# A written-out ramp for a fused attention and expert-FFN layer, with another order in its first four steps

## The reference

```
x = x + attention(layernorm(x), ctx, mask)     # x: 4 x 1024 x 256, ctx: 4 x 64 x 256
x = x + ffn(layernorm(x))

attention: q = query @ Wq + bq (16 heads of 16); k = ctx @ Wk + bk; v = ctx @ Wv + bv (one head, shared)
           softmax(q k / 4, masked) @ v, then @ Wo + bo
ffn:       xm = mix of each row with its two neighbours (3 taps per column)
           scores = tanh(xm @ Wo1 + bo1) @ Wo2 + bo2; expert = argmax over 9
           out = layernorm(x + (xm @ W1[expert] + b1[expert]) @ W2[expert] + b2[expert]) * gamma + beta
```

## Time and profile before

| | us |
|---|---|
| median of 3 runs | 359.27 |
| lowest and highest | 357.69, 359.3 |
| profiled execution, device time | 357.65 |
| its span | 355.8 |

### The profile page before, as it was taken

How to read it: one execution, slowest core, us unless ns; L and a number is a source line. 1 busy time by engine, 2 the same in 40 slices (tenths; PEclk the granted TensorE clock), 3 DMA queues, 4 the chain that set the end, 5 groups by cost and what they waited for, 6 DMA issues and landing times.

```text
span 355.8 us, 7313 instructions
## 1 busy us (share of the span) xinstructions
PE 312.0 (88%) x2700; PEld 230.7 (65%) x2700; DVE 282.4 (79%) x606; ACT 183.0 (51%) x285; POOL 188.2 (53%) x226
## 2 busy tenths in 40 slices
PE   1588788765999999999999999999999999799990
PEld 1374364452667957795678767876678568677980
DVE  2675398595769899889989898989798866689866
ACT  1452835625764477537851777258444752367400
POOL 0444002633178179944895299728881787164044
PEclk9998999996999999999999999999999999899996
DMA  7509500020002001200110010000100010001003
GB/s 210 177 0 218 106 0 1 2 76 0 0 4 76 0 2 62 73 3 0 59 52 22 0 59 0 0 0 2 61 0 2 2 61 2 0 0 62 3 0 118
DMA packets 20564, 13.44 MB, mean 38 GB/s; under 512 B 10097, under 2 KB 20282, under 8 KB 20538
## 3 DMA queue, kind: packets, MB, share of 16 engines
q1 hardware_dynamic: 18898, 12.53, 12.0%
q10 hardware_dynamic: 1640, 0.57, 0.7%
HBM read 8.90 MB, written 4.19 MB: 37 GB/s over the span
## 4 chain that ended last, share of the span: by engine, by line
PE 76%; DVE 12%; ACT 5%; issue 3%; POOL 2%; DMA 1%; DVEq 0%; ACTq 0%; POOLq 0%
PE ps L429 16%; PE ps L434 7%; PE ps L584 7%; PE ps L668 6%; PE ps L673 5%; PE ps L669 5%; PE ps L541 5%; PE ps L566 4%; PE ps L560 4%; DVE mx L1115 3%; DVE osb L1139 3%; PE ps L650 2%; PE ps L544 2%; PE ps L635 2%; PE ps L481 2%
## 5 line engine op out<-in xcount | busy, mean ns | idle before, releaser
L1408 POOL TENSOR_TENSOR rs<-ve,halfneg 128x4 f32<-128x4 f32 x24 | 26.7, 1113 | 106.8 <-DVE ve L1078 106.8
L843 ACT ACTIVATE e<-ps 128x1024 f32<-128x1024 f32 x32 | 31.1, 1024 | 20.3 <-PE ps L548 20.3
L1115 DVE TENSOR_REDUCE mx<-ps 128x16 f32<-128x1024 f32 x32 | 37.9, 1216 | 0.3 <-PE ps L516 0.3
L668 PE MATMUL ps<-w2h,hmh 128*128 128x256 f32 (+1 forms) x140 | 35.6, 288 | 0.0
L669 PE MATMUL ps<-w2l,hmh 128*128 128x256 f32 (+1 forms) x140 | 34.7, 283 | 0.0
L1465 POOL TENSOR_TENSOR hml<-hs,hmh 128x512 fp32r<-128x512 f32 x24 | 30.3, 1276 | 7.4 <-ACT hmh L904 7.3
L868 ACT ACTIVATE xh<-x,vb,rs 128x256 f32<-128x256 f32 x32 | 16.6, 591 | 33.5 <-POOL vb L1421 33.5
L584 PE MATMUL ps<-wo,osb 128*128 128x256 f32 x128 | 31.3, 390 | 2.0 <-DVE osb L1139 2.0
L894 ACT ACTIVATE hs<-ps,b1s 128x512 f32<-128x512 f32 x28 | 19.3, 689 | 24.4 <-PE ps L434 24.4
L1454 POOL TENSOR_TENSOR y<-xh2f,gms 128x256 f32<-128x256 f32 x28 | 22.2, 824 | 17.5 <-DVE xh2f L1087 17.5
L429 PE MATMUL ps<-xmh,w1h 128*128 128x512 f32 x80 | 27.8, 429 | 3.3 <-DVE xmh L1190 3.3
(11 more groups left out here) (161 smaller groups left out, 787.5 us busy)
## 6 DMA issues: line engine op xcount, KB each, us to landing
xin<-in_x SPq DMA_DIRECT2D x8, 512.0 KB, 4.1
out<-y SPq DMA_DIRECT2D x7, 512.0 KB, 2.9
min_<-in_mask_Bx1xSxS_ik SPq DMA_DIRECT2D x8, 128.0 KB, 4.8
hs<-in_L_ffn_W SPq DMA_DIRECT2D x2, 288.0 KB
y<-in_constants SPq DMA_DIRECT2D x1, 512.0 KB, 8.7
hs<-in_L_ffn_W SPq DMA_DIRECT2D x1, 512.0 KB
out<-xin SPq DMA_DIRECT2D x2, 256.0 KB, 2.2
cst<-in_constants SPq DMA_DIRECT2D x1, 384.0 KB, 6.0
```

Of the source, the lines that this page charges most:

```text
L668: nc.tensor.matmul(o, L.hi(m, r)[:, ks], w2h[0:r, m, :], start=(m == 0), stop=False)
L843: nc.scalar.activation(e[:, 2 * i:2 * i + 2, :], ps[:, bank:bank + 2, :], ACT.Exp).then_inc(s_e, 1)
L1115: v.tensor_reduce(mx[:, k, :].rearrange("p (a h) -> p a h", a=2), ps[:, bank:bank + 2, :].rearrange("p a (h s) -> p a h s", s=SK), AX.X, A ...
L1408: g.tensor_tensor(ln[7][:, :], ln[6][:, :], halfneg[:, :], ALU.pow).then_inc(s_r, 1)
```

## The change

It has these parts.

1. Start. ACT's queue loads Wq second, and bq is on a semaphore of its own. DVE takes the first layernorm's statistics ahead of the copies of the transposed context; ACT normalises two of the four tiles of chunk (0, 0) and DVE the other two. PE runs `t1(0, 0)` ahead of `keys()`, the mask last; DVE copies the keys after `x_lo`.
2. Step 1. `wq(0, 1)` and, on DVE between the second and the third maximum, `x_lo(0, 1)` move here from step 2 and from the end of the step.
3. FFN weights. SP issues their loads ahead of `next_inputs(0, 0)`. ACT's split of them goes from the end of step 2 to between the two exponential halves of step 2, and DVE's low parts from behind step 2 to its front.
4. Step 3. DVE applies the second layernorm of (0, 0) and (0, 1), at the ends of steps 2 and 3, in place of ACT. `early_mix` goes from the end of step 3 to its front, its high part behind `layernorm1_apply` on ACT and its low part on POOL ahead of `add_beta` and `add_bo`. On PE `wq(1, 0)` and `t2(0, 0)` keep their places ahead of the second scores; `t2(0, 1)` leaves the end of the step.
5. Step 4. PE runs scores half 0, `wq(1, 1)`, `t2(0, 1)` into banks 6 and 7, scores half 1 and only then `w1`. ACT copies the `t2` transposes, then makes the second exponentials and the query copy, and the `hidden` copies come behind them. DVE makes the last column behind the statistics of (2, 0).
6. All four engines' hardware loops are written out.

```diff
...
                 sp.wait_ge(s_ln1, at(b, NJ, j + 1))
+                if (b, j) == (0, 0):
+                    sp.wait_ge(s_ln1d, 1)
                 sp.wait_ge(s_xb, at(b, NJ, j + 1))
                 sp.dma_start(xin[:, j], xr[:, b + 1, j]).then_inc(s_x[j], 16)
...
+            load_ffn_weights()
             next_inputs(0, 0)
-            load_ffn_weights()
...
+            def mask_transposed(b, j, mask_bank):
...
+            def t1(b, j, bank, mask_bank=2):
+                first = (b, j) == (0, 0)
+                if first:
+                    pe.wait_ge(s_ln1d, 1)
+                else:
+                    mask_transposed(b, j, mask_bank)
                 pe.wait_ge(s_ln1, at(b, NJ, j + 1))
                 if mask_bank == 2:
...
+                if first:
+                    mask_transposed(b, j, mask_bank)
...
+            def wq(b, j, bank, first_f=False):
                 pe.wait_ge(s_xTl, at(b, NJ, j + 1))
-                if bank == 0:
+                if first_f:
+                    pe.wait_ge(s_x1, at(b, 2 * NJ, 2 * j - 2))
+                elif bank == 0:
                     pe.wait_ge(s_x2T, at(b, NJ * KD, (j - 1) * KD))
...
-            def t2(b, j, front, late):
+            def t2(b, j, bank=0):
                 pe.wait_ge(s_x1, at(b, 2 * NJ, 2 * (j + 1)))
-                if late:
-                    pe.wait_ge(s_nT, at(b, NJ, j + 2))
...
                 if n:
                     scores_transposed(*n, 0, front)
+                if late:
+                    wq(*front, fb, f)
+                    t2(*late, 6 if f else 0)
+                    scores_transposed(*n, 1, front)
                 if f:
                     w1(*f, 0)
                     w1(*f, 4)
+                if n and not late:
                     scores_transposed(*n, 1, front)
-                if front:
+                if front and not late and n != (0, 0):
                     wq(*front, fb)
-                if late:
-                    t2(*late, front, True)
-                if n and not f:
-                    scores_transposed(*n, 1, front)
                 if not n:
...
                     scores_for_max(*front, 2, banks)
                     scores_for_max(*front, 3, banks)
+                if not n:
+                    wq(*after, fb)
                 if n:
                     project_out(*n, (0, 1))
                 if f:
...
-                if n and (f or n[1] == NJ - 1):
-                    t2(*n, front, False)
+                if f:
+                    t2(*n)
...
             context_transposed()
+            t1(0, 0, 6)
             keys()
-            t1(0, 0, 6)
...
-            with pe.Fori(1, B - 1) as r:
-                step((r, 0), (r, 1), (r - 1, 0), (r + 1, 0))
+            for r in range(1, B - 1):
+                step((r, 0), (r, 1), (r - 1, 0), (r + 1, 0), (0, 1) if r == 1 else None)
                 step((r, 1), (r + 1, 0), (r - 1, 1), (r + 1, 1))
...
             load(ctx_in, ctx.rearrange("b s d -> s b d"), s_ctx)
+            load(wq32, Wq.rearrange("(c p) n -> p c n", p=P), s_wq)
             load(wk[:, :, :], Wk.rearrange("(c p) n -> p c n", p=P), s_wk)
             load(wv[:, :, :], Wv.rearrange("(c p) n -> p c n", p=P), s_wk)
             load(bks[:, :], bk.rearrange("(h p o) -> h p o", h=1, o=1).broadcast_to([P // DK, DK, 1]), s_wk)
             load(bvs[:, :], row_broadcast(bv, DK), s_wk)
-            load(wq32, Wq.rearrange("(c p) n -> p c n", p=P), s_wq)
-            load(bqs[:, :], bq.rearrange("(c p) -> p c", p=P), s_wq)
+            load(bqs[:, :], bq.rearrange("(c p) -> p c", p=P), s_bq)
...
-                for k in range(NT):
+                for k in range(NT // 2 if (b, j) == (0, 0) else NT):
...
                 if n:
                     softmax_exp(*n, 0)
+                if late and f:
+                    copy_t2(*late, 6)
+                    softmax_exp(*n, 1)
+                    q_copy(*front, 0)
+                elif late:
+                    copy_t2(*late)
+                    softmax_exp(*n, 1)
+                    q_copy(*front, 6)
                 if f:
                     hidden(*f, 0)
                     hidden(*f, 4)
-                if late:
-                    layernorm2_apply(*late)
-                    copy_t2(*late)
-                if n:
-                    softmax_exp(*n, 1)
-                if front:
-                    q_copy(*front, 0 if f else 6)
+                if n and n == (0, 0):
+                    split_ffn_weights()
+                if not late:
+                    if n:
+                        softmax_exp(*n, 1)
+                    if front:
+                        q_copy(*front, 0 if f else 6)
...
                 if after and not f:
                     layernorm1_apply(*after)
-                if n and n[1] == 0 and not f:
-                    split_ffn_weights()
+                if late and not f:
+                    early_mixed_hi(n[0])
...
-                if n and not f and n[1] == NJ - 1:
-                    layernorm2_apply(*n)
-                if n and (f or n[1] == NJ - 1):
+                if f:
                     copy_t2(*n)
-                if n and n[1] == NJ - 1 and not f:
-                    early_mixed_hi(n[0])
                 if after and f:
...
+            def first_layernorm1_upper():
+                dve.wait_ge(s_ln1b, 1)
+                for k in range(NT // 2, NT):
+                    a = v.tensor_scalar(xh1[:, k, :], xin[:, 0, k, :], ln1[7][:, k:k + 1], ln1[5][:, k:k + 1], ALU.mult, ALU.add)
+                a.then_inc(s_ln1d, 1)
+
+            def layernorm2_apply(b, j):
+                dve.wait_ge(s_ln2b, at(b, NJ, j + 1))
+                for k in range(NT):
+                    a = v.tensor_scalar(xh2[:, j, k, :], x1[:, j, k, :], ln2[7][:, k:k + 1], ln2[5][:, k:k + 1], ALU.mult, ALU.add)
+                a.then_inc(s_ln2, 1)
...
-            def step(n, front, f, after):
+            def step(n, front, f, after, late=None):
                 banks = banks_for_max(n, f)
-                if after and not f:
+                if after:
                     layernorm1_stats(*after)
-                if after and f:
-                    layernorm1_stats(*after)
+                if n and n == (0, 0):
+                    ffn_weights_lo()
+                if late and f:
+                    last_column(late[0])
+                elif late:
+                    dve.wait_ge(s_wf, 16 * WF_LOADS)
+                    early_mix(late[0])
                 if f and f[1] == 0:
                     second_mix(f[0])
...
+                if not n:
+                    x_lo(*after, 6)
...
-                if after:
+                if after and n:
                     x_lo(*after, 0 if f else 6)
                 if f:
                     layernorm3_apply(*f)
-                elif n and n[1] == NJ - 1:
-                    dve.wait_ge(s_wf, 16 * WF_LOADS)
-                    early_mix(n[0])
-                    last_column(n[0])
-
+                elif n:
+                    layernorm2_apply(*n)
+
+            layernorm1_stats(0, 0)
             transposed_context_copied()
-            layernorm1_stats(0, 0)
+            first_layernorm1_upper()
             memsets()
             key_weights_repeated()
-            keys()
             wq_lo()
             x_lo(0, 0, 6)
+            keys()
             step(None, (0, 0), None, (0, 1))
             step((0, 0), (0, 1), None, (1, 0))
-            ffn_weights_lo()
-            step((0, 1), (1, 0), None, (1, 1))
-            with dve.Fori(1, B - 1) as r:
-                step((r, 0), (r, 1), (r - 1, 0), (r + 1, 0))
+            step((0, 1), (1, 0), None, (1, 1), (0, 0))
+            for r in range(1, B - 1):
+                step((r, 0), (r, 1), (r - 1, 0), (r + 1, 0), (0, 1) if r == 1 else None)
                 step((r, 1), (r + 1, 0), (r - 1, 1), (r + 1, 1))
...
+                if n and n[1] == NJ - 1 and not f:
+                    early_mixed_lo(n[0])
...
-                elif n and n[1] == NJ - 1:
-                    early_mixed_lo(n[0])
...
```

More of the change, by code:

```diff
@@ L210, in layer_program @@
         s_ctx, s_wk, s_wq = sem("context_loaded"), sem("key_value_weights_loaded"), sem("wq_loaded")
+        s_bq = sem("bq_loaded")
         s_wo_in, s_wf = sem("wo_loaded"), sem("ffn_weights_loaded")
@@ L225, in layer_program @@
         s_ln3v, s_ln3r, s_ln3 = sem("ln3_var"), sem("ln3_rstd"), sem("ln3_done")
+        s_ln1d = sem("first_ln1_upper_tiles")
         s_mb, s_xb = sem("mask_bias"), sem("x_plus_bo")
@@ L594, in t2 @@
                     for k in range(NT):
-                        mm = nc.tensor.transpose(ps[:, c, k * P:(k + 1) * P], xh2[:, j, k, c * P:(c + 1) * P], ident)
+                        mm = nc.tensor.transpose(ps[:, bank + c, k * P:(k + 1) * P], xh2[:, j, k, c * P:(c + 1) * P], ident)
                     mm.then_inc(s_x2p, 1)
@@ L802, in _ @@
             load(bvs[:, :], row_broadcast(bv, DK), s_wk)
[L803 to L804 removed]
```

(22 more changed lines are left out.)

3 lines of the change are left out of this document (removed).

## The result

The changed kernel takes 347.35 us (median of 4 runs, 345.63 to 349.92), against 358.48 us for the kernel before on the same chip (4 runs, 354.67 to 359.3). The ratio on record is 0.9707, with a 95% interval of 0.9666 to 0.9748: faster by 2.9% (the quotient of the two medians alone is 0.969). The forecast was 349.8 us in 346.5 to 354.0. The profiled execution took 348.3 us with a span of 346.5, where the forecast for it, without the 0.8 for the median, was 349.05. Its span is 9.3 us shorter than the 355.8 of before.

A forecast was written before the change was run, and what follows sets the result against it. PE was taken to bound the kernel from 97 us on, behind a ramp where no engine is full. -0.6 + 1.9 + 1.3 + 6.0 = 8.6 off 357.65 gives 349.05; plus 0.8, 349.8 us, range 346.5 to 354.

The forecast's parts named there:

- The start (A): Start through step 1, to the transposed maxima of (0, 0): a loss of 0.6 us, at best a gain of 1.3.
- The rival of the start that loses more: Start: Wq's load takes turns with x, which lands at 9.5; a loss of 2.9 us, time 352.1; 7 in 100.
- Step 2 (B): Transposed maxima to second exponentials of step 2: 6.98 us instead of 8.86, a gain of 1.9.
- a rival that would come after the change: Step 2: with wq gone PE has gaps and its clock falls, costing about 3 us, time 353; 13 in 100.
- The second layernorm (C): Step 3: with the layernorm on DVE, PE's 1.34 us wait for ACT before t2(0, 0) goes; a gain of 1.3.
- Step 4 (D): Step 4's new order brings the gate to 92.5 from 98.52: a gain of 6.0 us, 7.0 if hidden weren't behind.
- The loops (E): Hardware loops written out: taken as 0, with bounds 0 and a gain of 0.3 us in all.
- The median: Median of runs was 1.6 us above the profiled run before; half of it, 0.8, was added to the forecast.
- The best bound of the prediction: Whole kernel: 346.0 us from the profiled run if the start gains 1.3, step 4 7.0 and the loops 0.3.
- POOL did come later: Early low part delays POOL's additions and the load of x(2, 0); 2 us lost, time 351.8; 13 in 100.
- The slower case: Clock stays low from step 2 through step 3; slower than before, 370 if all of it; 4 in 100.

The follow-up runs named there:

- e2: Changed kernel with the late transposes, their copies and the last column back at the end of step 3, step 4 in old order; 351.2 us, ratio 0.9805.
- e1: Kernel before with only its four hardware loops written out; 358.46 us, ratio 0.9997.
- e9: Changed kernel with the second layernorm of (0, 0) on ACT again, that of (0, 1) staying on DVE; one run, 348.3 us.
- e12: Changed kernel with the old start and with wq(0, 1) back between the scores of step 2; one run, 349.56 us.
- e7: Changed kernel with ACT's split of the FFN weights moved from between step 2's exponential pairs to the end of step 1; one run, 346.2 us.
- e3: Changed kernel with ACT's copies of the late transposes put behind the second exponentials and query copy in step 4; 353.83 us, ratio 0.9878.
- e10: Changed kernel with the early mix back at the end of step 3, step 4 keeping its new order; one run, 354.43 us.
- e4: Changed kernel with hidden copies 0 and 4 ahead of the query copy in step 4; one run, 348.71 us.
- e11: Changed kernel executed once more, nothing changed; one run, 348.75 us.
- e8: Changed kernel with ACT's weight split at the end of step 1 and the first two hidden copies ahead of step 4's query copy; 346.59 us, ratio 0.9687.
- e5: Changed kernel with the old start: old load order, context copies, first layernorm on ACT, keys ahead of t1; one run, 349.92 us.
- e6: Changed kernel with wq(0, 1) back in step 2 ahead of the second scores and x_lo(0, 1) behind step 1's maxima; one run, 349.1 us.

## Why the prediction was right

**The start (A), predicted -0.6, measured -0.3.** x was there at 6.49, not at 7.2 as taken, and the keys ended at 15.7, not at 16.4. The rival of the start that loses more did not come. By the rule of the Trainium skill, DMA: Bandwidth & Descriptors, Queues, rings and completion order, Wq as the second load of ACT's queue should take turns with x. Of the start's two x loads the faster landed in 5.3 us and the slower in 8.8, where the kernel before had 5.4 and 8.3, and e2, with the new order of loads too, 5.3 and 7.8: a cost of such turns isn't seen on the first load, and nothing waits for the second. The 0.3 measured is itself no more than the difference between two executions: the transposed maxima come at 28.30 and 28.95 with the old start (before, e1), and at 28.59 to 29.03 with the new one, but for e9's 29.46, where a low clock lies ahead of them.

**Step 2 (B), predicted +1.9, measured +1.9, for a reason that was only half right, and so in part by luck.** The new chain was 6.95 us by the trace against 6.98 worked out. But I took the 8.86 us of before as what the order costs. Of it some 1.5 us were work at the lower clock: 3.51 us to the first exponentials against 2.45, and 1.19 us for the product's first pair against 0.73. The measured gain is mostly that this is gone (e12). I had that clock in view as a rival that would come after the change, and did not see that it stood in the term I subtracted from. The price of the split, 0.85, was wrong as well: it is 0.15 to 0.3, since PE needs 2.17 us behind the first exponentials and not 1.65 (e7). The row of the scores with their banks free, 1.14, does not stand for the same scores behind a wait for banks, 2.04. The sum held because the split and PE's chain end together. It is the reading of one execution, too: with the changed kernel's program up to there the chain took from 6.69 (e3) to 7.63 us (e10), by where the low clock lay, which makes B anything from 1.2 to 2.2.

**The second layernorm (C), predicted +1.3, measured +1.4**, and 1.2 when it was undone (e9).

**Step 4 (D), predicted +6.0, measured +6.1.** The third `w1` waited 0.85 for `hidden` where 1.0 was predicted, and e4 shows that it was this and nothing else. The gate is 14.9 us behind `t1`'s start, where it was 21.1. Some 0.9 of the 6.1 are clock here as well: before, the late transposes ran in 1.94 us, with the clock low from 80.4 to 87.2, and the copies, the mix's low part and the first `w1` followed from them. That share the prediction had in view, since it counted them at 1.06 after the change. e2, e3 and e10 show what the term is made of: its parts can't be priced one by one and added.

**The loops (E), predicted 0, measured 0** (e1). The Trainium skill, Runtime: NRT & Kernel Launch, Instruction fetch mechanics, has a taken branch break the sequential prefetch. No such cost is seen here: with the four loops of two rounds written out it is 257.4 us from the gate to the end, against 257.3.

**The median.** I could not tell whether the 1.6 us between the profiled run of before and its median would stay, and added half. The profiled run came out at 348.3, 0.75 under the 349.05 of the sum, of which A gives 0.3, C and D 0.1 each and the part behind the gate another 0.1 to 0.2. The median came out at 347.35, 2.4 us under the forecast: it lies 0.95 under its profiled run, where that of before lay 0.8 to 1.6 over its own. So the medians are 11.1 us apart, where the sum had 8.6 and the profiled runs 9.3; that the 349.8 lies within 2.5 us of the result rests on the sum, and the rest is spread that it did not model. The last section has a likely reason, stretches at the lower clock that one execution has and another lacks. The best bound of the prediction is off by a little: 357.65 less 1.3, 1.9, 1.3, 7.0 and 0.3 is 345.85, not 346.0.

**The rivals.** POOL did come later against the rest, and it cost nothing: it released x(2, 0) at 74.58 against 73.54, with everything else ahead by 3, so 4 us late where the rival had 2.6. The load landed in 3.6 us, at 78.2, and DVE took it at 79.54; with the 6.8 us of the start's loads it would have been late. The clock did fall in step 2, at 34 to 37.6, but most of it lay under exponentials and query copy: it stretched mask and maxima products by 0.4 us, of which ACT's split hid 0.2. Where it began up to 0.8 us earlier it cost more: against the changed kernel 0.4 us in e11 and 0.7 in e10, and in e8 1.0 against e7, which lacks it. The rival's 3 us never came. The slower case asked for a clock that stays low through step 3; each fall in steps 1 and 2 ended within 5 us. Where PE had stood still for over 4 us ahead of it (e3, e10) it lasted 7 and 10 us, though in e2, behind 4.28 us, only 3.4. In e3 and e10 it cost 1.1 us (6.58 from the first `w1` to the gate against 5.51, which holds the wait of 0.85 that e3 hasn't; against e4's 4.63 it is 1.9) and some 2.6 (12.2 from the first exponentials of step 4 to the gate, against the 9.6 expected).

## What to carry to other kernels

Before a distance in the trace is taken as the cost of an order, look at the granted clock in it: a stretch of 4 us at half rate can be the gain or the loss. When work is moved into a gap, the move often pays only together with the one that empties the place ahead of it: here one half of the rearrangement alone was worse than none (by the clock that fell in its gap), and the other alone gave a third of it. And an engine at half load can hold the most valuable order in the kernel, since what counts is which of its calls the full engine waits for.

## What the runs showed of the hardware

From the gate to the end the kernels fall in two groups. With a stretch of low clock some 47 to 43 us before the end it is 257.1 to 257.5 us (before, after, e1, e4, e5, e6, e8, e11, e12); without it 255.3 to 255.5 (e2, e3, e7, e9, e10). The program of the last steps is the same in all of them. Busy time by stretch, of the changed kernel and of e7, from 48 to 40 us before the end:

```profile
...
298.50:302.50 4.00, 2.97 (x9) 2.42 (x10) 3.47 (x12) 0.69 (x1) 1.01 (x1) 0.77 0.00 0
302.50:306.50 4.00, 3.88 (x18) 2.92 (x16) 3.02 (x7) 2.32 (x4) 1.35 (x2) 0.81 0.00 0
...
```

```profile
...
296.40:300.40 4.00, 1.80 (x11) 1.36 (x10) 3.44 (x15) 1.09 (x2) 1.01 (x1) 1.00 0.00 0
300.40:304.40 4.00, 3.83 (x21) 2.93 (x19) 3.89 (x9) 2.84 (x5) 0.00 (x0) 1.00 0.00 0
...
```

One such stretch of about 4 us costs 1.8 us here. It comes behind a gap of PE (busy 0.33 us from 297 to 299 in the changed kernel, which waits 2.19 us for DVE there), but not always: e7 has the same gap, 2.20 us, and no fall. That would account for much of the spread of 345.6 to 349.9 us between runs of the changed kernel, whose spans of 346.5, 344.6 and 343.8 go with mean clocks of 0.983, 0.987 and 0.992, and why e2 and e9 look better by their time than at the gate. What decides whether it comes in an execution, I can't say.

The second thing is what DVE and GpSimd do to each other. In step 2 GpSimd's four additions took 2.82 us before, with DVE idle at their side, and 4.04 us beside DVE's low parts of the weights, of which the first took 1.99 us against 1.49 where it ran ahead of the additions (e7). Timeline of the changed kernel:

```profile
...
32.71 4.04 POOL L1474 TENSOR_TENSOR x<-xin,bos 128x256 f32<-128x256 f32 x4
...
34.17 1.99 DVE L1075 TENSOR_TENSOR w1l<-hs,w1h 128x1280 fp32r<-128x1280 f32 x1 [2.57 <-ACT w1h L829]
...
```

The Trainium skill, SBUF — State Buffer, Who interferes with whom, has the two engines share a pair of ports under an exclusive lock, and the rows agree: both were slower side by side. That a lock is the reason they can't show. Neither was on the chain here: ACT's split and PE's scores set the second exponentials.
